# Seven of eight groups of the expert layer's logits computed inside the second cross attention

## The reference

```
x = _layernorm(x + minGRU(x))                      # 4 gated recurrent layers
x = _layernorm(x + cross_attention_0(x, ctx))      # with a temperature from three features
x = _layernorm(x + tile_ffn(x))
x = _layernorm(x + self_attention(x))
x = _layernorm(x + cross_attention_1(x, ctx))      # 16 heads of 8
x = _layernorm(x + experts(x))
```

```
hs = x.reshape(-1, H)
logits = hs @ w_gate                               # 4096 x 8
probs = softmax(logits); best = argmax(probs)
gate = probs of the best; only the first 100 tokens of an expert are kept
out = gate * (hs @ w_expert + b_expert)
```

## Time and profile before

| | us |
|---|---|
| median of 3 runs | 1846.4 |
| lowest and highest | 1839.13, 1853.87 |
| the profiled execution | 1854.84 |
| its span | 1853.1 |
| PE busy | 1646.3 (89%) |
| DVE busy | 1260.1 (68%) |
| ACT busy | 1202.8 (65%) |
| POOL busy | 481.8 (26%) |
| mean granted clock of TensorE | 0.933 |

### The profile page before, as it was taken

One profiled execution on the slowest core, in us unless ns is written; L12 is line 12 of the kernel. 1 busy time (PEld: TensorE's weight loads), 2 busy tenths in 40 slices (PEclk: granted clock), 3 DMA queues, 4 the chain that ended last, 5 costly groups with the idle time before them and its releaser, 6 DMA issues. The chain is left out here.

```text
span 1853.1 us, 28867 instructions
## 1 busy us (share of the span) xinstructions
PE 1646.3 (89%) x10524; PEld 949.1 (51%) x10524; DVE 1260.1 (68%) x1701; ACT 1202.8 (65%) x2569; POOL 481.8 (26%) x402
## 2 busy tenths in 40 slices
PE   5999999999999964888879798999999999789985
PEld 2343444444444422666656535666666566466654
DVE  2778777777777767888815555666666666588854
ACT  3787887787787743788772365555655556377754
POOL 2111011111111134777620002222222222155530
PEclk9999999999999975899995689999999999799977
DMA  3000001000000021000000000000000000000001
GB/s 131 1 12 1 0 7 24 0 0 0 1 0 1 0 48 30 5 6 9 2 2 1 0 1 1 1 1 1 1 1 1 1 1 1 8 8 8 2 1 46
DMA packets 30529, 16.99 MB, mean 9 GB/s; under 512 B 8545, under 2 KB 29246, under 8 KB 30398
## 3 DMA queue, kind: packets, MB, share of 16 engines
q1 hardware_dynamic: 27710, 10.52, 2.3%
q10 hardware_dynamic: 2688, 4.72, 0.7%
HBM read 13.14 MB, written 2.10 MB: 8 GB/s over the span
## 5 line engine op out<-in xcount | busy, mean ns | idle before, releaser
L2247 POOL TENSOR_TENSOR self_probs<-self_probs,self_rz 128x1024 f32<-128x1024 f32 x64 | 121.3, 1895 | 488.9 <-DVE self_rz L2278 488.9
L558 POOL TENSOR_SCALAR gru_decay<-gru_zgate 128x512 f32<-128x512 f32 x96 | 75.2, 783 | 563.1 <-ACT gru_zgate L509 537.1
L2222 ACT ACTIVATE self_probs<-self_scores,self_neg 128x128 f32<-128x128 f32 x512 | 181.4, 383 | 16.8 <-DVE self_neg L2273 16.8
L417 PE MATMUL gru_gate<-gru_xn,gru_whg 128*128 128x512 f32 x384 | 182.2, 597 | 3.5 <-DVE gru_xn L605 3.5
L421 PE MATMUL gru_hid<-gru_xn,gru_whg 128*128 128x512 f32 x384 | 180.4, 592 | 0.0
L429 PE MATMUL gru_out<-gru_y,gru_wo 128*128 128x512 f32 x384 | 178.1, 599 | 0.7 <-DVE gru_y L635 0.6
L1385 ACT ACTIVATE x_pt<-x_turned 77x512 f32<-77x512 f32 x256 | 137.6, 585 | 60.3 <-PE x_turned L1282 59.0
L1282 PE MATMUL x_turned<-const_ident,x_probs 128*77 128x128 f32 x1024 | 147.5, 290 | 20.8 <-POOL x_probs L1434 11.5
L1282 PEld LDWEIGHTS x_turned<-const_ident,x_probs 128*77 128x77 f32 x1024 | 119.6, 154 | 73.2 <-POOL x_probs L1434 25.9
L630 DVE SCALAR_TENSOR_TENSOR gru_ghid<-gru_hid,gru_half_c,gru_sighid 128x512 f32<-128x512 f32 x96 | 71.7, 747 | 107.9 <-ACT gru_sighid L510 107.8
L1491 DVE TENSOR_REDUCE x_m<-x_scores 128x16 f32<-128x1232 f32 x64 | 91.7, 1432 | 49.9 <-PE x_scores L1271 48.6
(11 more groups left out here) (440 smaller groups left out, 3507.7 us busy)
## 6 DMA issues: line engine op xcount, KB each, us to landing
gru_whg<-in_L_attn_Whg ACTq DMA_DIRECT2D x4, 768.0 KB, 9.5
x0e_ctx_in<-in_ctx SPq DMA_DIRECT2D x16, 154.0 KB
gru_xin<-in_x SPq DMA_DIRECT2D x8, 256.0 KB, 2.9
out<-moe_y SPq DMA_DIRECT2D x8, 256.0 KB, 2.2
gru_wo<-in_L_attn_Wo ACTq DMA_DIRECT2D x4, 384.0 KB, 10.6
selfe_raw<-in_L_attn_Wq SPq DMA_DIRECT2D x1, 512.0 KB, 4.5
selfe_raw<-in_L_attn_Wk SPq DMA_DIRECT2D x1, 512.0 KB, 5.7
selfe_raw<-in_L_attn_Wv SPq DMA_DIRECT2D x1, 512.0 KB, 6.8
```

Source lines behind the costliest of these rows:

```text
L417: mm(ps_gate[n % 2][:, :], whg[:, l, k, DI + c * P:DI + (c + 1) * P], xn[u][:, k, :], start=(k == 0), stop=(k == KH - 1))
L2222: last = f(probs[n % 2][:, a, jj, :], ps_s[n % 2][:, a, jj * T:(jj + 1) * T], ACT.Exp, bias=neg[n % 2][:, a, jj:jj + 1], accum_out=z[n % 2 ...
L2247: pool.tensor_tensor(probs[n % 2][:, :, :, :], probs[n % 2][:, :, :, :], whole, ALU.mult).then_inc(pn_ready.sem, 1)
```

## The change

The logits of groups 0 to 6 are made in the second cross attention. In slot n with r = 1, ahead of the scores, PE makes the four sequences of group n // 4 - 2, writes them into columns 308 to 339 of the scores' first bank, which the scores leave free, and counts `l_mm`. It waits for the group's `xT_ready`, for `d_ready` as the scores do (since the bank is the one that DVE reads), and for the copy before. The slots are n = 9, 13, 17, 21, 25 and 29, and n = 33 for group 6, where there are no scores any more. DVE copies the 32 columns to a new SBUF tile between the maximum and the difference of the same slot, for group 6 by itself. Group 7 stays in the expert stage; DVE copies it too, and reads all the logits from SBUF. The first cross attention gets no such steps.

```diff
+    def score(self, nc, xT, g, bank):
+        for n in range(g * GB, (g + 1) * GB):
+            at = n % GB * EXPERTS
+            last = nc.tensor.matmul(bank[:, at:at + EXPERTS], xT[:, n * T:(n + 1) * T], self.wg[:, :], start=True, stop=True)
+        last.then_inc(self.l_mm.sem, 1)
+    def keep(self, nc, g, bank):
+        to = self.logits[:, g * GB:(g + 1) * GB, :].rearrange("p b e -> p (b e)")
+        nc.vector.tensor_copy(to, bank[:, 0:GB * EXPERTS]).then_inc(self.l_kept.sem, 1)
...
+                ORDER += [("logits", g - 2, 0)] * (r == 1 and experts is not None)
                 ORDER += [("scores", n, 0), ("kbd", n + 1, 0), ("weigh", n - 1, 0)]
...
+        spare = ps_s[:, 0, TILE4 * S:]
+        beside = {GB * (g + 2) + 1: g for g in range(NG - 1) if GB * (g + 2) + 1 < B} if experts else {}
...
+                    elif kind == "logits":
+                        if n == 0:
+                            pe.wait_ge(experts.loaded.sem, experts.n_loads * DMA)
+                        pe.wait_ge(xT_ready.sem, n + 1)
+                        pe.wait_ge(d_ready.sem, min(GB * (n + 2) + 1, B))
+                        if n:
+                            pe.wait_ge(experts.l_kept.sem, n)
+                        experts.score(nc, xT, n, spare)
...
                         v.tensor_reduce(top, scored(), AX.X, ALU.max).then_inc(m_ready.sem, 1)
+                        if n in beside:
+                            dve.wait_ge(experts.l_mm.sem, beside[n] + 1)
+                            experts.keep(nc, beside[n], spare)
                         dve.wait_ge(m_ready.sem, n + 1)
...
-                for n in range(B):
-                    last = mm(ps_l[:, n, :], seq(n), wg[:, :], start=True, stop=True)
-                last.then_inc(l_mm.sem, 1)
+                early.score(nc, xT, NG - 1, ps_l)
...
-                dve.wait_ge(l_mm.sem, 1)
-                link(v.tensor_reduce(top[:, :], ps_l[:, :, :], AX.X, ALU.max))
-                v.tensor_tensor(probs[:, :, :], ps_l[:, :, :], wide(top), ALU.subtract).then_inc(dist_ready.sem, 1)
+                dve.wait_ge(early.l_mm.sem, NG)
+                early.keep(nc, NG - 1, ps_l)
+                dve.wait_ge(early.l_kept.sem, NG)
+                link(v.tensor_reduce(top[:, :], logits[:, :, :], AX.X, ALU.max))
+                v.tensor_tensor(probs[:, :, :], logits[:, :, :], wide(top), ALU.subtract).then_inc(dist_ready.sem, 1)
```

More of the change, by code:

```diff
@@ L1029, in load @@
             sp.dma_start(dst, src, allow_slow_non_contiguous=True).then_inc(self.loaded.sem, DMA)
+EXPERTS, CAPACITY = 8, 100
 class ExpertEarly:
@@ L1039, in __init__ @@
         self.be = t.sb("be", [P, GB, D])
+        self.logits = t.sb("logits", [P, B, EXPERTS])
+        self.l_mm = t.count("l_mm")
+        self.l_kept = t.count("l_kept")
         self.src = (w_gate, w_expert, b_expert)
@@ L1057, in cross_attention, with cross_attention_stage @@
     const["stages"].append((arguments, more))
-def cross_attention_stage(nc, const, early, later, next_cross, tag, xT, context, temper):
+def cross_attention_stage(nc, const, early, later, next_cross, experts, tag, xT, context, temper):
     with ExitStack() as ctx:
@@ L1197, in cross_attention_stage @@
         PER_SEQ = ("scores", "pre", "turn", "sums", "attend", "logs", "scale", "soft", "exp", "kbd", "weigh")
-        ORDER = [s for s in ORDER if 0 <= s[1] < (B if s[0] in PER_SEQ else NG)]
+        ORDER = [s for s in ORDER if 0 <= s[1] < (B if s[0] in PER_SEQ else NG - 1 if s[0] == "logits" else NG)]
+        spare = ps_s[:, 0, TILE4 * S:]
+        beside = {GB * (g + 2) + 1: g for g in range(NG - 1) if GB * (g + 2) + 1 < B} if experts else {}
         MISC = {}
@@ L1494, in _ @@
                                         top.unsqueeze(3).broadcast_to([P, TILE4, TILE4, S]), ALU.subtract).then_inc(d_ready.sem, 1)
+                    elif kind == "logits" and n not in beside.values():
+                        dve.wait_ge(experts.l_mm.sem, n + 1)
+                        experts.keep(nc, n, spare)
                     elif kind == "sums":
@@ L2306, in self_attention_stage @@
         t.clear_counts()
-EXPERTS, CAPACITY = 8, 100
 def moe_ffn(nc, const, xT, w_gate, w_expert, b_expert, out):
@@ L2322, in moe_ffn @@
     early_experts = ExpertEarly(nc, ctx, w_gate, w_expert, b_expert)
-    cross_attention_stage(nc, const, first, (early_tiles, early_own, second, early_experts), second, *cross0[0][:3], temper=True)
+    cross_attention_stage(nc, const, first, (early_tiles, early_own, second, early_experts), second, None, *cross0[0][:3], temper=True)
     second.hold(ctx)
@@ L2328, in moe_ffn @@
         self_attention_stage(nc, const, early_own, first.vpad, second, xT)
-    cross_attention_stage(nc, const, second, (), None, *cross1[0][:3], temper=False)
+    cross_attention_stage(nc, const, second, (), None, early_experts, *cross1[0][:3], temper=False)
     moe_ffn_stage(nc, const, early_experts, xT, out)
@@ L2344, in moe_ffn_stage @@
         HELD = NG - NR
-        wg, we, be = early.wg, early.we, early.be
+        we, be = early.we, early.be
         we_mean = t.sb("we_mean", [P, 1])
@@ L2363, in moe_ffn_stage @@
         var, logs, inv = (t.sb(n, [P, B]) for n in ("var", "logs", "inv"))
-        ps_l = t.ps("logits", [P, B, EXPERTS])
+        ps_l = t.ps("logits", [P, GB * EXPERTS])
+        logits = early.logits
         ps_p = t.ps("places", [P, 2, NE])
@@ L2370, in moe_ffn_stage @@
         shaped = t.count("shaped")
-        l_mm = t.count("l_mm")
         we_ready = t.count("we_ready")
```

## The result

The changed kernel takes 1856.6 us in the median (1847.9 to 1866.3, 11 runs) against 1846.4 before; the ratio of the kernels, run by run, is 1.0044, 95% interval 1.0023 to 1.0065. It is slower by some 8 us, inside the forecast's range and inside the 1% that counts as no change, but well above the 1847 I put as the likeliest, and only 1.4 us under the range's upper end. The runs of the kernel before lie in two bunches, 1839 to 1847 and 1849 to 1859 us, so that a median or a ratio can shift by some us with how many runs fall into each.

The account below looks back on a forecast made before the run. TensorE's gapless chain was taken as the bound: -11.4 gain, +4.7 rounds, +0.4 sixth group, +1.85 tail make -4.4 us; clock falls of +4.4 to +6.6 bring 0.0 to +2.2, so 1847 us, range 1837 to 1858.

Parts of the forecast that it names:

- The gain: Start of the expert stage: with 56 of 64 logits passes moved away, PE's turns start 11.4 us earlier.
- rival 4: Expert stage boundary: clock rises a group later or DVE's routing delays the places; gain 9.2, 1849 to 1851 us; chance 0.08.
- The price without the clock: Second cross attention: five rounds (sequences 9 to 25) each cost 0.94 us, 4.7 us together.
- The sixth group: Ahead of sequence 29 in the second cross attention: its logits cost 0.4 us.
- The tail: End of the cross attention: the seventh group's logits delay the turns by 1.85 us, all exposed.
- The clock, the term that failed: Cross attention rounds: 2.1 us of waiting and eight-column matmuls make two to three clock falls, +4.4 to +6.6 us.
- rival 3: Cross attention: the clock falls in every round and low-clock PE bounds the stage; +14.1 us, 1860 us; chance 0.12.
- The likeliest case: Whole kernel: the clock falls in some rounds, not all; 1847 us, own range 1844 to 1851; chance 0.5.
- The clock holds: Cross attention: the clock does not fall; sum -4.4 us, 1842 us; chance 0.22.
- The work hides: Cross attention: DVE or POOL, not PE, sets the round, 0.4 us a group; sum -7.1 us, 1839 us; chance 0.08.
- DVE's cover of the copy: Cross attention round: 2.6 us cover DVE's 2.2 us lateness with a 0.25 us copy; at 0.60 just used up.
- The sign that I had named: Cross attention round: DVE's 1.67 us wait for PE's scores gets smaller.

Follow-up runs that it names:

- gain-alone: Changed kernel without logits in the cross attention, group 7's copied over the other groups, whose own are left out; ratio 0.9909 to the kernel before.
- other-place: Changed kernel with the logits in the attention output's bank behind the keys' matmul, where PE waits for POOL anyway, ACT copying; ratio 0.9926 to the kernel before.
- filled version: Changed kernel with three useless 204-column matmuls put in front of PE's wait for xT; ratio 0.9986 to the kernel before.
- wait alone: Kernel before with only the new wait for xT ahead of the scores, logits left in the expert stage; ratio 1.0012 to the kernel before.
- no-wait: Changed kernel making the logits of the group three before instead of two before, so PE does not stand for xT; ratio 0.9944 to the kernel before.

## Why the prediction was right, and what it sized wrongly

**The gain** of 11.4 us for PE's turns is nearly what the trace has, 11.3 (13.65 - 2.37; I had taken the end of the logits' row for the start of the turns, whose row begins 0.14 earlier). By the stage's length it is 10.5, as the clock stayed down 1.6 us longer behind the first turn; rival 4 had this as a whole group and 9.2. It is 11.0 and 11.1 in the gain-alone and the other-place runs.

**The price without the clock.** 0.94 us a round was forecast; the filled version measures 1.03. The difference is the eight passes, 0.99 us and not the 0.89 taken from the experts' matmuls. The wait alone costs 0.04 and the matmuls alone nothing; only in a row do they exceed the 1.1 us that POOL and the keys' input give. The copy was to cost nothing on DVE at 0.25; its row is 0.18 and it costs nothing.

**The sixth group** was too cheap at 0.4 us. I let PE's wait of 1.87 us for POOL take back the delay, though the scores that come late there make POOL's next product late too. The second wait for POOL behind sequence 29's scores, first in the gain-alone version and then in the filled one:

```profile
1772.68 1.10 PE L1312 MATMUL x_turned<-const_ident,x_probs 128*77 128x128 f32 x8 [0.88 <-POOL x_probs L1464]
```

```profile
1770.81 1.10 PE L1314 MATMUL x_turned<-const_ident,x_probs 128*77 128x128 f32 x8 [1.93 <-POOL x_probs L1466]
```

It grows by 1.05 us. By the starts of the scores the group costs some 1.9 us: up to sequence 31's scores the filled version has lost 7.1 us against the gain-alone one, leaving out the 1.66 us of a fall near the stage's start, and five rounds at 1.03 account for 5.2 of it.

**The tail.** 1.85 forecast. From sequence 31's scores to the next stage the filled version takes 25.65 us against 24.16 before and 23.22 in the gain-alone version, 1.5 or 2.4; the three have different stretches at clock 0.50 there, so that it can't be told closer. The change takes 27.7, because a fall at 1796.2 comes on top.

**The clock, the term that failed.** "I expect falls in some rounds, not all": two to three at 2.2 us each. There were six, one beside every group of logits that stands ahead of scores, and a seventh at the tail's group. The price was about right: 24.70 - 23.05 = 1.65 for a short one, 25.93 - 23.05 = 2.9 for a long one, the five rounds 126.6 - 5 x 23.05 = 11.4 us together, 2.3 each. So of the 22.2 us, 16.9 lie in the five rounds (126.6 against 109.7 before): 5.6 for the queue, which is what the filled version's 5 x 23.05 has over before, and 11.4 for the clock. The stretch ahead adds 4.0 (2.1 for the first wait and logits, most of the rest a fall near 1615 that comes before any logits and that the wait-alone, no-wait and filled versions show too), the end 3.5, and between the scores of sequences 29 and 31 2.2 come back: the kernel before took 12.86 us there with the fall of the earlier trace rows, the gain-alone version 10.48 without one, and the change 10.64, with a fall of its own that took the place of waits (PE waits 0.34 us for POOL up to there, in the gain-alone version 1.88 and 0.88). The mechanism of rival 3 came true, at 3.4 us a round where it had 4.65. With 3.4 its own sum would be +7.9 (5 x 3.4 + 0.4 + 1.85 - 11.4); the +11.7 of the profiles has on top, in the main, what I left out: the fall near 1615, the fall at the tail and the gain's missing 0.9. I had compared the hole of 2.1 us with the 1.87 that made the clock fall and the 0.65 that did not, and then hedged; the nearest row said fall.

**Luck.** That the time lies in the range is in part luck. The range's upper end cut rival 3 in half, rival 3 is what happened in every round, and 1856.6 is 1.4 us short of that end. The likeliest case, 1844 to 1851, did not come.

**The rivals.** The clock holds: refuted by every round. The work hides: true of each half alone, not of the sum. That DVE's cover of the copy would be used up: it was not, DVE waits 1.98 and 2.25 us for the scores. The sign that I had named, the wait of 1.67 us getting smaller, did not come in the change, where the slow turns delay the next scores; at full clock it did. In the filled version the wait is 0.61:

```profile
1699.90 1.44 DVE L1523 TENSOR_REDUCE x_m<-x_scores 128x16 f32<-128x1232 f32 x1 [0.61 <-PE x_scores L1303]
```

## What to carry to other kernels

A few microseconds of work moved from an exposed stage into a loop have two prices: what they delay, and what the engine does meanwhile. Before counting a wait as swallowed, add the stretch in which TensorE stands and the stretch of its narrow matmuls, and compare the sum with the stretches in the trace behind which the clock fell. Here 1.1 us of standing was enough in two slots of six and 2.1 us of both in six of six, so between the two it can go either way. If the sum lies there, take data that is ready earlier, or move the work to a wait that exists anyway: here the same seven groups cost 3.4 us a round in one place and nothing in two others.

## What was not expected of the hardware

Three matmuls of 204 columns whose result nobody reads, put where TensorE stood for 1.11 us, made rounds of 24.7 to 25.9 us into 23.05. And 1.8 us of back-to-back eight-column matmuls lowered the clock with the engine busy all the time by its rows (1.8 us without a gap; 21.7 of 22.6 us in a round), just as 13.8 us of them had not raised it.
